# Attention maxima in a two-layer transformer kernel: eight of them issued beside the second half's projections, the rest issued in pairs on half steps

## The reference, cut to what matters

```python
def _L1_attn_ref(x, rby, Wq, bq, Wk, bk, Wv, bv, Wo, bo, ln_gamma, ln_beta):
    x = x + _pos_encoding(S, d, yellow)[None, :, :]
    Q, K, V = (proj(Wq, bq), proj(Wk, bk), proj(Wv, bv))
    logits = jnp.einsum('bhqd,bhkd->bhqk', Q, K) / scale
    logits = logits * scale_matrix
    attn = jax.nn.softmax(logits, axis=-1)
    out = jnp.einsum('bhqk,bhkd->bhqd', attn, V) * (1.0 + yellow * eps_adaptive)
    ...
    return normalized * gamma_rby + ln_beta
```

## Time and profile before

| | |
|---|---|
| median of 3 runs | 2490.08 us (2489.07 to 2490.46) |
| the profiled execution's own time | 2490.05 us |
| its span, first to last instruction | 2488.1 us |
| PE busy | 2087.6 us, 84% |
| DVE busy | 1937.4 us, 78% |
| ACT busy | 1424.7 us, 57% |
| POOL busy | 600.0 us, 24% |
| chain that ended last | PE 41%, DVE 37%, ACT 15%, issue 5% |
| mean granted TensorE clock | 0.934 of full speed |

### The profile page before, as it was taken

The page is one execution under the profiler, slowest core; times in us unless marked ns, Lnnn a source line. Parts: engine busy times, 40 slices in busy tenths (PEclk is TensorE's granted clock), DMA queues, the critical chain, the costliest instruction groups (busy, mean ns, idle before and its releaser), DMA issues.

```text
span 2488.1 us, 48854 instructions
## 1 busy us (share of the span) xinstructions
PE 2087.6 (84%) x18320; PEld 1228.3 (49%) x18320; DVE 1937.4 (78%) x4231; ACT 1424.7 (57%) x2618; POOL 600.0 (24%) x480
## 2 busy tenths in 40 slices
PE   5997789787799688978789958987788995888876
PEld 3674233556467323355647723336464772334645
DVE  7756997887755799788785579977878458997786
ACT  4343577748334377784733437767563343776765
POOL 2632000432253100134134210021505330004050
PEclk9998899999899799999989969999998996999999
DMA  4002100100000210011000030010100003001010
GB/s 155 1 1 64 41 11 6 34 21 19 18 1 1 77 31 8 15 26 32 16 9 1 1 90 20 7 27 16 32 13 9 1 5 87 20 10 35 5 33 21
DMA packets 63892, 63.25 MB, mean 25 GB/s; under 512 B 22000, under 2 KB 49200, under 8 KB 63152
## 3 DMA queue, kind: packets, MB, share of 16 engines
q1 hardware_dynamic: 60472, 57.27, 9.2%
q10 hardware_dynamic: 3192, 2.90, 0.4%
HBM read 24.68 MB, written 15.01 MB: 16 GB/s over the span
## 4 chain that ended last, share of the span: by engine, by line
PE 41%; DVE 37%; ACT 15%; issue 5%; DMA 1%; SPq 0%; DVEq 0%; ACTq 0%
PE PS L1388 40%; DVE arena L1136 18%; ACT arena L750 9%; DVE arena L1236 2%; DVE s_at L1211 1%; DVE arena L1204 1%; DMA tmp<-xf 1%; ACT arena L697 1%; DVE tmp L1211 1%; PE PS L1406 1%; ACT arena L758 1%; DVE arena L1329 1%; ACT arena L718 1%; ACT tmp L704 1%; ACT arena L720 1%
## 5 line engine op out<-in xcount | busy, mean ns | idle before, releaser
L1388 PE MATMUL PS<-arena 128*32 128x256 f32 (+5 forms) x11328 | 797.6, 325 | 165.5 <-DVE arena L1136 72.2
L1388 PEld LDWEIGHTS PS<-arena 128*32 128x32 f32 (+5 forms) x11328 | 368.6, 118 | 594.9 <-DVE arena L1136 293.0
L1136 DVE TENSOR_REDUCE arena<-PS 128x1 f32<-128x512 f32 x1024 | 639.5, 683 | 18.7 <-PE PS L1388 18.2
L697 ACT ACTIVATE arena<-PS 128x1024 f32<-128x1024 f32 x512 | 519.1, 1028 | 196.7 <-PE PS L1388 196.3
L652 ACT ACTIVATE arena<-PS 128x512 f32<-128x512 f32 x256 | 150.7, 597 | 245.2 <-PE PS L1388 245.0
L1388 PEld LDWEIGHTS PS<-w2e,arena 128*128 128x128 f32 x2048 | 246.0, 192 | 50.0 <-issue 49.7
L1098 DVE TENSOR_TENSOR arena<-PS,arena 128x512 f32<-128x512 f32 x128 | 86.4, 689 | 214.5 <-PE PS L1388 214.1
L1388 PE MATMUL PS<-w2e,arena 128*128 128x128 f32 x2048 | 247.5, 275 | 0.1
L750 ACT ACTIVATE arena<-PS,arena 128x128 f32<-128x128 f32 x512 | 236.4, 626 | 0.0
L503 POOL TENSOR_TENSOR zz<-zz,arena 128x512 f32<-128x512 f32 x104 | 135.1, 1299 | 271.3 <-DVE arena L1098 242.8
L1388 PE MATMUL PS<-wqkv,arena 128*128 128x512 f32 x384 | 176.8, 598 | 21.7 <-ACT arena L732 21.7
(11 more groups left out here) (306 smaller groups left out, 3267.0 us busy)
## 6 DMA issues: line engine op xcount, KB each, us to landing
arena<-arena SPq DMA_DIRECT2D x120, 128.0 KB, 2.3
scr_q<-arena SPq DMA_DIRECT2D x40, 128.0 KB, 2.4
scr_k<-arena SPq DMA_DIRECT2D x40, 128.0 KB, 2.4
arena<-scr_k SPq DMA_DIRECT2D x24, 200.0 KB
arena<-scr_q SPq DMA_DIRECT2D x24, 192.0 KB
scr_m<-arena SPq DMA_DIRECT2D x256, 1.0 KB
x_in<-in_x SPq DMA_DIRECT2D x5, 512.0 KB, 4.7
arena<-scr_m SPq DMA_DIRECT2D x128, 2.0 KB
```

The source lines that it names most:

```text
L697: act.activation(pb[:, n % 8], pair(2 * (n % 2)), ACT.Exp).then_inc(S["p"], 1)
L1136: dve.tensor_reduce(mxp[:, blk % 2, j, t, hf:hf + 1], PS[:, ring_bank(m), :], AX, ALU.max)\
L1388: return pe.matmul(o, w, v, start=start, stop=stop, **kw)
```

## The change

It has five parts.

1. **Eight early maxima.** `maxima(0, 4)` stands between the second half's transposes (`rows_of(1)`) and `project(1)`, `maxima(4, 8)` between `project(1)` and `values_of(1)`. They use banks 4 to 7. A wait on `ym` is added before the first. The transposes of `xn2` stand behind maxima 8 to 11 and wait for VectorE to have reduced eight.
2. **VectorE's order** becomes: `values_in(0)`, memsets, maxima 0 to 3, `rest` of q, maximum 4, `rest` of k, `third(1)`, maximum 5, `values_in(1)`, maxima 6 and on.
3. **ScalarE's order** in `project`: q's bf16 cast stands right behind q's evacuation, before k's evacuation.
4. **Pairs on half steps.** `ahead` counts half steps: a pair can stand before a step's scores or behind them.
5. **Run-ahead from 34 to 28.** 111 pairs are spread over 228 half steps instead of one for each step from step 0, so the last pair moves from step 110 to behind the scores of step 113. When the last pair is issued the maxima are 28 ahead of two for each step, where they were 34 ahead.

```diff
+EARLY_MAX = 8
...
         def ring_bank(m):
 
-            return m % 6 if m < maxima_by(0) else 5 + m % 3
+            return 4 + m % 4 if m < EARLY_MAX else m % 6 if m < maxima_by(0) else 5 + m % 3
...
-        def ahead(n):
-
-            return AHEAD + 2 * n
+        def ahead(h):
+
+            return min(MAXIMA, AHEAD + 2 * (h * (MAXIMA - AHEAD) // (4 * (STEPS - T - 6))))
...
+                    act.wait_ge(S["qkf"], 2 * hf + 1)
+                    act.copy(qk3[:, 0, 0, cols], qkf[:, 0]).then_inc(S["bf1"], 1)
                     act.wait_ge(S["k_ps"], hf + 1)
                     act.activation(qkf[:, 1], PS[:, up_bank("k", hf, 0), :], ACT.Identity, bias=res["bk"][:, 0:1])\
                         .then_inc(S["qkf"], 1)
-                    for qk in range(2):
-                        act.wait_ge(S["qkf"], 2 * hf + qk + 1)
-                        act.copy(qk3[:, qk, 0, cols], qkf[:, qk]).then_inc(S["bf1"], 1)
+                    act.wait_ge(S["qkf"], 2 * hf + 2)
+                    act.copy(qk3[:, 1, 0, cols], qkf[:, 1]).then_inc(S["bf1"], 1)
...
+                for m in range(4):
+                    maximum(m)
+                rest(1, (0,))
+                maximum(4)
+                rest(1, (1,))
+                third(1)
+                maximum(5)
+                values_in(1)
+                for m in range(6, MAXIMA):
+                    maximum(m)
...
                         if m == 0:
+                            pe.wait_ge(S["ym"], 2 * LOOPS * E)
                             pe.wait_ge(S["qs_early"], 16 * 4)
...
+                rows_of(1)
+                maxima(0, 4)
+                project(1)
+                maxima(4, EARLY_MAX)
+                values_of(1)
+                pe.wait_ge(S["vaug"], 2)
+                pe.wait_ge(S["qkf"], 4)
...
-                maxima(0, 6)
+                maxima(EARLY_MAX, EARLY_MAX + 4)
                 pe.wait_ge(S["xn2"], T)
+                pe.wait_ge(S["mx"], EARLY_MAX)
                 transposes(xn2, 6, None, "hT_ps")
-                maxima(6, maxima_by(0))
+                maxima(EARLY_MAX + 4, maxima_by(0))
...
-                        maxima(ahead(n), ahead(n + 1))
+                        maxima(ahead(2 * n), ahead(2 * n + 1))
...
                         ins.then_inc(S["st_ps"], 1)
+                        maxima(ahead(2 * n + 1), ahead(2 * n + 2))
```

More of the change, by code:

```diff
@@ L1074, in values_in, with rest @@
                         .then_inc(S["vaug"], 1)
-                def rest(hf):
-                    for qk in range(2):
+                def rest(hf, which=range(2)):
+                    for qk in which:
                         dve.wait_ge(S["bf1"], 2 * hf + qk + 1)
@@ L1126, in _, with maximum @@
                 values_in(0)
-                rest(1)
-                values_in(1)
-                third(1)
                 link(dve.memset(mtop[:], 0.0))
                 dve.memset(hT[64:P, 0:1], 0.0).then_inc(S["hT_late"], 1)
-                for m in range(MAXIMA):
+                def maximum(m):
                     blk, t, s, hf = max_at(m)
@@ L1137, in _ @@
                         .then_inc(S["mx"], 1)
+                for m in range(4):
[8 more added lines that the diff above has]
+                    maximum(m)
+                    blk = max_at(m)[0]
                     if m + 1 == maxima_by(blk):
@@ L1584, in _ @@
                         down(k, e)
-                rows_of(1)
-                project(1)
-                values_of(1)
-                pe.wait_ge(S["vaug"], 2)
-                pe.wait_ge(S["qkf"], 4)
                 def maxima(lo, hi):
```

## The result

| | before | after |
|---|---|---|
| median beside each other | 2490.46 us (five runs, 2489.07 to 2490.88) | 2475.99 us (four runs, 2474.57 to 2476.91) |
| profiled span | 2488.1 us | 2473.0 us |
| mean granted TensorE clock | 0.934 | 0.939 |
| wait ahead of VectorE's maxima, all 1024 | 18.7 us | 28.1 us |

The ratio is 0.9942, with a 95% interval of 0.9926 to 0.9958: the change saves 14.5 us by the medians and 14.4 by the ratio. A fifth run of after, at a lower granted clock (0.842), took 3712.64 us and is left out of both; with it the median is 2476.89. The forecast was 2475 us. The profiles are of one execution each (2490.05 us before, 2475.08 after).

A forecast was written before the change was run, and what follows sets the result against it. VectorE's maxima were taken to bound the kernel, with TensorE setting the last steps. Per iteration 1.4 + 0.2 - 1.6 + 0.8 + 3.0 = 3.8 us, 15 us for four, from 2490 to 2475 us; range 2463 to 2486.

The forecast's parts named there:

- What bounds the kernel: VectorE's maxima set the time from 240.8 to 411 us; the last steps behind them run at TensorE's pace.
- Early part, 1.4 us: Eight early maxima fill VectorE's wait before the steps; 1.4 us an iteration left at maximum 24, ends 0.5 and 2.9.
- the 242.5 that I gave as a sign: Sign of being right: eight reductions done before 242.5 us in the profile after.
- my upper end of 2.9: Early part's largest gain, 2.9 us, if the copies don't hold ScalarE's loads and only VectorE's own order counts.
- One cold pair less: Ahead of the steps, the half-clock stretch of scores, products and pairs begins a pair earlier: 0.2 us gained.
- Half steps: Steps 1 to 113: 1.6 us lost at three moves and two skipped pairs, 0.8 back from bank 4 waits.
- the rule that a pair d us late costs VectorE d us: In the steps, a pair d us late delays VectorE by d, since only one reduction is in hand.
- Tail, 3.0 us: Behind the last pair, 14 scores and 15 products remain instead of 18 and 18: 3.0 us shorter.
- The 1.0 us of room at step 120: Block 15's maxima should be in `QS` 1.0 us before step 120 needs them, so the shorter run-ahead costs nothing.
- The clock as a gain: Early pairs behind the projections could hold full clock through to the steps: 1.5 to 2.7 us an iteration, 2467 total.
- only the tail gains: Rival: early maxima's gain is given back at maximum 16, 0 instead of 1.4, 2480 to 2482; 0.15 with large losses (2483 to 2488).
- rival three: Half steps cost more than they save: TensorE's step outgrows VectorE's 1.25 us, up to 2507 us; chance 0.09.

The follow-up runs named there:

- the aligned version: The changed kernel with the pairs' moves between before and behind the scores placed only behind a block's first pair; 2463.80 us, ratio 0.9874 to 0.9905 to before.
- the early part alone: The changed kernel with pairs back on whole steps and run-ahead back at 34, leaving the eight early maxima and new engine orders; 2488.08 us.

## Why the prediction was right, point by point

The time, 2475 us, was within 1 us (2475.99), but that closeness is luck, since two errors cancel: attention gained 20.0 us instead of 15, and 4.9 us were lost where the sum had nothing. The mechanism of the attention's three stages was right; the term furthest off is the net of the half steps, where I had 0.8 us lost in an iteration and 0.2 were gained.

- **What bounds the kernel: right.** The maxima run on VectorE with small waits from the early part to the end, and a microsecond taken from the early part or from the tail shows in the stage.
- **Early part, 1.4 us: 2.0.** My times hang on transposes at 230.69, and these start at 231.42 in after, so I count from their start. The first reduction came at 1.7 us, as worked out; the eighth ended at 11.6 (241.78 and two of 0.60), where I had 11.5, though on the trace's own clock that is 243.0 and past the 242.5 that I gave as a sign; the writes had landed at 13.3 instead of 13.0. The last load was issued at 14.2 (245.60), just before my 14.3 to 14.8, and its pair started 2.8 us behind it instead of 3.2. Together they put maximum 16 at 17.0 us, where I had 17.4 to 18.0, and that is the 0.6 us. Its wait for the DMA from scratch was right. The step that failed is the one behind my upper end of 2.9: the copies do hold ScalarE's loads, by 0.4 to 0.5 us in three iterations of after, but in the aligned version nothing was gained with them out of the way. What holds maximum 16 there is the way through scratch itself, and in after at most 0.2 to 0.3 us more.
- **One cold pair less, 0.2 us gained: 0.2 lost.** From maximum 24 to the full clock after has waits of 0.59, six of 0.17, 0.72 and 0.37, 2.70 us, before 0.31, six of 0.17, 0.71 and 0.45, 2.49. One pair fewer was there, but maxima 26 and 27 now have a wait of 0.17 that they had not, and the first wait had grown from 0.31 to 0.59.
- **Half steps, 1.6 us lost and 0.8 back: 0.2 back.** The two skipped pairs cost 0.51 each, near what I worked out (0.46). The three moves behind the scores cost less than 0.21: in step 19 it fell together with the copy's wait, 0.46 where 0.55 were due, and in steps 57 and 95 no wait is listed. By the starts of the reductions the pair is 0.10 us late in step 95, and in step 57 not at all, where a block's closing operations stand before it. So less is lost than the rule that a pair d us late costs VectorE d us gives from my 0.21; slack on VectorE was one of the ends that I named. The waits of 0.34 went at steps 35, 67 and 99, as I said, and also at 83, behind a block's closing operations. What stands in the steps is 0.46 + 0.51 + 0.34 + 0.51 = 1.82 us, before 6 x 0.34 = 2.04.
- **Tail, 3.0 us: 3.0**, 18.00 to 15.01. The 1.0 us of room at step 120 is 0.8 to 0.9: with one step fewer the row comes 0.06 us late in the first iteration, with two 0.9.
- **The clock as a gain: wrong.** It was to stay full behind the projections. In after it is 1.00 at 238, 0.78 at 240 and 0.50 from 242, so it falls as before. Its price in the prediction is misread too: six cold pairs wait 0.17 there, not nine; with the other three waits it is 2.49 us, inside the 1.5 to 2.7 that I gave. The Trainium skill (TensorE: Matmul & The Clock Gate, Part 1: The HAM clock gate) says that the throttled state is the default and that activity releases it. In the run with extra matmuls a TensorE shown as fully busy from 254 to 260 stayed at 0.50, so in this trace that work did not release it before the steps.
- **What was missing.** No term and no rival stood for the clock outside attention. It took 4.2 us here, and where 5.8 us of delay were added to before, all else grew by 11.4, the 5.8 included. The rival "only the tail gains" (the copies, transposes and loads move) and the growth in the half steps of rival three did not happen: 2.0 of 2.0 us of the early part arrive at maximum 24, and from step 19 to 37 no wait on VectorE is listed but the one of 0.46.

Those 0.7 us at the start say nothing about the change: the version with the early part alone has the same program up to there, and its transposes start at 229.98 us by the same account; those of the version with run-ahead 24, again the same up to there, start at 233.46.

## What to carry over

Where one engine has a long row of equal operations, look first at what waits in front of it and behind it: the tail here could be worked out to a tenth of a microsecond from two durations and a count of steps, and the room in front of the next wait to two tenths. Put changes of rhythm where the bound engine has other work for a moment (here a block's closing operations), and they cost little (a skipped pair 0.2 us instead of 0.5). And where TensorE changes its clock, don't add stage gains to a total: cut the program at events that both kernels share, and see what the untouched stretches took back.

## What the runs showed of the hardware

- The response to a change of time in one place is not its size. A delay of 0.72 us in each iteration cost 6.4 us (3.5 to 8.5) where 2.9 were added, 1.44 cost 14.3 and 14.0 where 5.8 were. The stretches at half clock lay elsewhere in after than in before.
- A stage that was 5.7 us shorter in four iterations (769.1 against 774.8) left the median where it was within the intervals (2465.17 and 2463.80).
- The same 12 matmuls of 128x512 in f32, behind the same wait of 2.19 us, took 5.42 us or 7.11, and both in one execution of the aligned version. The stretch around them, in untouched code, was 1.6 to 1.7 us longer with the 7.11 (411.8 against 410.1 and 410.2).
- Extra matmuls that keep TensorE busy (2.00 of 2.00 us) did not raise the granted clock from 0.50 in the windows from 254 to 260 us of the first iteration.
